# Routing the last token group in two halves, the other groups ahead of the last projections

## The reference

```python
# linear attention, 16 heads of 16, 64 features a head
q_prime = relu(q @ Wqf.T); k_prime = relu(k @ Wkf.T)
kv = einsum('bhnf,bhne->bhfe', k_prime, v)
out = einsum('bhmf,bhfe->bhme', q_prime, kv) / (qk_sum + 1e-8)
x = x + out @ Wo.T + bo
# mixture of experts on layernorm(x): 32 experts, top 6
scores = softmax(x2d @ wg_router.T)
topk_w, topk_idx = top_k(scores, 6)
pos = cumsum(one_hot(flat_idx)) - 1          # place of a token in its expert
xe = zeros(E, C, D).at[flat_idx, pos].add(x_rep)
ye = (silu(xe @ w_gate) * (xe @ w_up)) @ w_down
y = sum over k of ye[...] * topk_w  +  shared expert(x2d)
```

## Time and profile before

| | |
|---|---|
| median of 3 runs | 2223.54 us (2222.8 to 2228.28) |
| profiled execution | 2246.44 us |
| its span, first to last instruction | 2244.7 us |
| busy: PE, DVE, ACT, POOL | 1942.7, 1366.5, 1076.1, 718.4 us |
| mean granted TensorE clock | 0.929 |
| the last three groups of the LA | 784 to 967 us |
| last DVE instruction of the LA to the first gate product | 966.55 to 978.46 us |

### The profile page before, as it was taken

How to read it: one execution, slowest core, us unless ns; L and a number is a source line. 1 busy time by engine, 2 the same in 40 slices (tenths; PEclk the granted TensorE clock), 3 DMA queues, 4 the chain that set the end, 5 groups by cost and what they waited for, 6 DMA issues and landing times. The chain is left out here.

```text
span 2244.7 us, 41989 instructions
## 1 busy us (share of the span) xinstructions
PE 1942.7 (87%) x11797; PEld 1302.7 (58%) x11798; DVE 1366.5 (61%) x3452; ACT 1076.1 (48%) x2800; POOL 718.4 (32%) x691
## 2 busy tenths in 40 slices
PE   7999999998998999977899999889766789888655
PEld 4666666665555666644676666545433457677433
DVE  6555656665776344545343344679789447777687
ACT  5545545453333222102344444367588337666575
POOL 3332332330000014451465556523100026566310
PEclk9999999999999888878999999999888889899787
DMA  8960000000000001151678776400010111111100
GB/s 305 307 185 0 0 0 0 0 1 0 0 0 1 1 15 60 57 187 63 143 167 170 166 175 116 102 1 2 11 49 1 65 34 33 31 38 31 31 17 22
DMA packets 145575, 145.10 MB, mean 65 GB/s; under 512 B 49376, under 2 KB 133568, under 8 KB 145344
## 3 DMA queue, kind: packets, MB, share of 16 engines
q1 hardware_dynamic: 122432, 113.81, 17.1%
q0 software_dynamic: 23040, 30.01, 7.8%
HBM read 137.12 MB, written 66.44 MB: 91 GB/s over the span
## 5 line engine op out<-in xcount | busy, mean ns | idle before, releaser
L1686 POOL DMA_INDIRECT expert_sums<-moe_rows_in,moe_to x128 | 198.0, 1547 | 151.6 <-DMA expert_sums<-moe_rows_in,moe_to 79.2
L1949 DVE COPY moe_ht_e<-moe_turned 128x256 f32<-128x256 f32 x128 | 54.4, 425 | 203.3 <-PE moe_turned L1767 178.3
L1759 PE MATMUL moe_gate<-moe_places,moe_xt 128*128 x512 | 175.9, 466 | 2.1 <-issue 1.9
L619 ACT ACTIVATE ga_prob<-ga_score,ga_neg_max 128x128 f32<-128x128 f32 x256 | 99.8, 392 | 145.7 <-DVE ga_neg_max L493 145.7
L3012 POOL TENSOR_TENSOR wa_low<-wa_low,wa_top 128x512 f32<-128x512 f32 x128 | 133.2, 1041 | 97.7 <-DVE wa_top L3216 96.4
L240 POOL TENSOR_TENSOR ga_q_inv<-ga_q_sum,half 128x4 f32<-128x4 f32 x64 | 64.5, 1008 | 304.2 <-DVE ga_q_sum L476 304.2
L2039 POOL TENSOR_TENSOR ln_rstd<-ln_var,half 128x4 f32<-128x4 f32 (+1 forms) x16 | 21.9, 1370 | 370.8 <-DVE ln_var L2035 370.7
L1153 POOL DMA_INDIRECT slot_x<-early x96 | 94.3, 982 | 115.2 <-DVE early L1144 76.8
L3213 DVE SCALAR_TENSOR_TENSOR wa_low<-wa_score,early 128x512 f32<-128x512 f32 x128 | 87.8, 686 | 61.1 <-PE wa_score L3052 58.6
L375 PE MATMUL ga_summed<-ga_wo,ga_out_t 128*128 128x256 f32 x512 | 122.5, 383 | 0.7 <-ACT ga_out_t L627 0.7
L375 PEld LDWEIGHTS ga_summed<-ga_wo,ga_out_t 128*128 128x128 f32 x512 | 98.1, 192 | 40.6 <-issue 29.2
(11 more groups left out here) (480 smaller groups left out, 4969.4 us busy)
## 6 DMA issues: line engine op xcount, KB each, us to landing
moe_places<-in_L_ffn_packed SPq DMA_DIRECT2D x128, 608.0 KB
slot_x<-zeros SPq DMA_DIRECT2D x24, 1076.0 KB, 14.9
moe_rows_in<-slot_x SPq DMA_DIRECT2D x128, 134.5 KB
wa_v<-v_ctx SPq DMA_DIRECT2D x16, 180.0 KB, 3.0
early<-in_L_xattn_Wq SPq DMA_DIRECT2D x5, 512.0 KB, 7.8
x<-in_x SPq DMA_DIRECT2D x4, 512.0 KB, 9.3
ga_wo<-in_L_xattn_Wo SPq DMA_DIRECT2D x1, 2048.0 KB, 14.3
expert_sums<-zeros SPq DMA_DIRECT2D x2, 1024.0 KB, 8.6
```

The lines of the kernel that those rows point to most:

```text
L619: last = act.activation(prob[:, n % 2, part], score[:, n % 2, part], ACT.Exp, bias=neg_max[:, n % 2, h:h + 1], accum_out=total[:, n % 2, h ...
L1686: pool.indirect_dma_start(out=mem.sums[j % SUMS], out_offset=bass.IndirectOffsetOnAxis(ap=to[:, j:j + 1], axis=0), in_=y[:, j, :], in_offs ...
L1759: last = pe.matmul(both[j % 2][:, 0:2 * FE], xt[:, j % 2, c, :], packed[:, place, c * 2 * FE:(c + 1) * 2 * FE].rearrange("p a n -> p (a n) ...
```

## The change

- The last group's routing is split in spans of two tiles: `SPANS` has the three groups of four tiles and two of two tiles each (tiles 12, 13 and tiles 14, 15). All steps of the router take a span where they took a group.
- The first half of the last group is scaled after the last `normalize` of the LA, ahead of the last `update`; PE transposes it ahead of the last `sum_up` and computes its logits behind it; DVE softens it at the end of the LA. Its `exp`, `choose`, `pick`, `rank` and `find_slots` stand at the head of MoE, beside the second half's transposes and logits. The second half's `rank` stands after u = 1, and its `find_slots` after the first multiplication.
- In the other groups, transposes come after f = 0 and f = 1 (before: 3 and 5), the logits after f = 4 (before: behind all projections), `exp` on ACT after the Relu of f = 6 (before: after the last), `choose` ahead of the first tile's values, `pick` behind the first tile's pairs and `find_slots` behind the second's (before: `choose`, `pick`, `find_slots` behind the pairs of the tiles 0, 1 and 2).
- `EARLY_ROWS` is 11 instead of 10: POOL scatters eleven tiles in the LA. The root of tiles 12 and 13 stands ahead of tile 10's scatters, that of tiles 14 and 15 behind them.

The diff, cut; the steps left out only take the span's size in place of `GROUP`:

```diff
-EARLY_ROWS = (GROUPS - 1) * GROUP - 2
+EARLY_ROWS = (GROUPS - 1) * GROUP - 1
+SPANS = [(g * GROUP, (g + 1) * GROUP) for g in range(GROUPS - 1)] + [(B - GROUP, B - GROUP // 2), (B - GROUP // 2, B)]
+SPAN_OF = [n for n, (a, b) in enumerate(SPANS) for t in range(a, b)]
...
     def group(self, a, g):
-        return a[:, g * GROUP:(g + 1) * GROUP]
+        return a[:, SPANS[g][0]:SPANS[g][1]]
...
     def root(self, pool, g):
-        a, b = g * GROUP, (g + 1) * GROUP
+        a, b = SPANS[g]
         pool.wait_ge(self.var_ready.sem, self.var_ready.at(g))
-        pool.tensor_tensor(self.rstd[:, a:b], self.var[:, a:b], self.mem.half[:, 0:GROUP], ALU.pow).then_inc(self.rooted.sem, 1)
...
-        if n >= 2:
-            pe.wait_ge(self.lated.sem, self.lated.at(n // 2 - 1))
+        if GROUP <= 2 * n < B - GROUP // 2:
+            pe.wait_ge(self.lated.sem, self.lated.at(SPAN_OF[2 * n] - 1))
...
     def logits(self, pe, g):
-        pe.wait_ge(self.moved.sem, self.moved.at(2 * g + 1))
+        a, b = SPANS[g]
+        pe.wait_ge(self.moved.sem, self.moved.at(b // 2 - 1))
         if g >= 1:
-        for i in range(GROUP):
-            t = g * GROUP + i
+        for i in range(b - a):
+            t = a + i
...
-        pe.wait_ge(self.moved.sem, self.moved.at(2 * g + 1))
-        out = self.pairs[:, 0:GROUP * NE]
+        a, b = SPANS[g]
+        pe.wait_ge(self.moved.sem, self.moved.at(b // 2 - 1 if b <= B - GROUP else B // 2 - 1))
+        if b == B:
+            pe.wait_ge(self.lated.sem, self.lated.at(g - 1))
+        out = self.pairs[:, 0:(b - a) * NE]
...
+        if t in [a for a, b in SPANS]:
+            pool.wait_ge(self.placed.sem, self.placed.at(SPAN_OF[t]))
         if 1 <= t <= EARLY_ROWS:
             pool.wait_ge(self.mem.scattered[(t - 1) % SCATTERS].sem, 16 * TOPK * ((t - 1) // SCATTERS + 1))
...
                 for t in range(EARLY_ROWS):
                     if t % TG == 1 and t // TG < G - 2:
                         router.root(pool, t // TG + 1)
+                    if t == EARLY_ROWS - 1:
+                        router.root(pool, G - 1)
                     router.scatter(pool, t)
-                router.root(pool, G - 1)
+                router.root(pool, G)
...
                         m, part = divmod(f, FC // HC)
                         pe.wait_ge(moved.sem, moved.at(t * NP + m))
                         project(t, 2 * HC + f, [(w.fq[:, part * P:(part + 1) * P], qt[:, m, :])])
-                        if g >= 0 and f == 3:
+                        if g >= 0 and f == 0:
                             router.turn(pe, 2 * g)
-                        if g >= 0 and f == 5:
+                        if g >= 0 and f == 1:
                             router.turn(pe, 2 * g + 1)
-                    if g == 0:
-                        pe.wait_ge(route_loaded.sem, 16)
-                    if g >= 0:
-                        router.logits(pe, g)
+                        if g == 0 and f == 4:
+                            pe.wait_ge(route_loaded.sem, 16)
+                        if g >= 0 and f == 4:
+                            router.logits(pe, g)
...
                             turn_row(t * TG + j)
                         if j >= 1:
                             turn_mixed(t, j - 1)
-                        if g >= 0 and j == 2:
+                        if g >= 0 and j == 1:
                             router.rank(pe, g)
                     sum_up(t, TG - 2)
                     mix_up(t, TG - 1)
                     turn_mixed(t, TG - 1)
+                    if t == G - 1:
+                        router.turn(pe, 2 * t)
                     sum_up(t, TG - 1)
+                    if t == G - 1:
+                        router.logits(pe, t)
...
-                        if g >= 0 and n == 2 * HC + 3:
+                        if g >= 0 and n == 2 * HC:
                             router.move(act, 2 * g)
-                        if g >= 0 and n == 2 * HC + 5:
+                        if g >= 0 and n == 2 * HC + 1:
                             router.move(act, 2 * g + 1)
-                    if g >= 0:
-                        router.exp(act, g)
+                        if g >= 0 and n == 2 * HC + 6:
+                            router.exp(act, g)
...
+                    if t == G - 1:
+                        router.move(act, 2 * t)
...
                     for j in range(TG):
                         if g >= 0 and j == 0:
                             router.soften(dve, g)
+                            router.choose(dve, g)
                         features_values(t, j)
                         if j >= 2:
                             update(t, j - 2)
+                        if t == G - 1 and j == TG - 1:
+                            dve.wait_ge(counted.sem, counted.at(t * TG + 1))
+                            router.variance(dve, t)
                         if j >= 1:
                             normalize(t, j - 1)
                         pairs(t, j)
                         if g >= 0 and j == 0:
-                            router.choose(dve, g)
+                            router.pick(dve, g)
                         if g >= 0 and j == 1:
-                            router.pick(dve, g)
-                        if g >= 0 and j == 2:
                             router.find_slots(dve, g)
                     update(t, TG - 2)
                     normalize(t, TG - 1)
+                    if t == G - 1:
+                        router.shifts(dve, t)
+                        router.scale(dve, t)
                     update(t, TG - 1)
                 dve.wait_ge(counted.sem, counted.at(B - 1))
-                router.variance(dve, G - 1)
-                router.shifts(dve, G - 1)
-                router.scale(dve, G - 1)
+                router.variance(dve, G)
+                router.soften(dve, G - 1)
+                router.shifts(dve, G)
+                router.scale(dve, G)
...
-                router.turn(pe, 2 * LASTG)
                 router.turn(pe, 2 * LASTG + 1)
-                router.logits(pe, LASTG)
+                router.logits(pe, LASTG + 1)
+                router.rank(pe, LASTG)
                 pe.wait_ge(loaded.sem, 16 * len(loads))
                 for u in range(U):
                     gate_up(u)
                     if u == 1:
-                        router.rank(pe, LASTG)
+                        router.rank(pe, LASTG + 1)
                         router.counts(pe)
...
-                router.move(act, 2 * LASTG)
+                router.exp(act, LASTG)
                 router.move(act, 2 * LASTG + 1)
-                router.exp(act, LASTG)
+                router.exp(act, LASTG + 1)
...
-                router.soften(dve, LASTG)
                 router.choose(dve, LASTG)
                 router.pick(dve, LASTG)
+                router.soften(dve, LASTG + 1)
+                router.find_slots(dve, LASTG)
+                router.choose(dve, LASTG + 1)
+                router.pick(dve, LASTG + 1)
                 for u in range(U):
                     multiply(u)
                     if u == 0:
-                        router.find_slots(dve, LASTG)
+                        router.find_slots(dve, LASTG + 1)
```

More of the change, by code:

```diff
@@ L1048, in scale @@
     def scale(self, dve, g):
-        for t in range(g * GROUP, (g + 1) * GROUP):
+        for t in range(*SPANS[g]):
             dve.tensor_scalar(self.mem.xn[:, t, 0:H], self.mem.x[:, t, :], self.rstd[:, t:t + 1], self.shift[:, t:t + 1],
@@ L1094, in choose @@
         self.then(dve, dve.reciprocal(total, total))
-        self.then(dve, dve.tensor_tensor(prob, prob, total.unsqueeze(2).to_broadcast([P, GROUP, NE]), ALU.mult))
-        for t in range(g * GROUP, (g + 1) * GROUP):
+        self.then(dve, dve.tensor_tensor(prob, prob, total.unsqueeze(2).to_broadcast([P, size, NE]), ALU.mult))
+        for t in range(*SPANS[g]):
             n = self.did(dve.max(self.top[:, t, :], self.prob[:, t, :]))
         dve.wait_ge(self.step.sem, n)
-        for t in range(g * GROUP, (g + 1) * GROUP):
+        for t in range(*SPANS[g]):
             n = self.did(dve.max_index(self.index[:, t, :], self.top[:, t, :], self.prob[:, t, :]))
@@ L1127, in find_slots @@
     def find_slots(self, dve, g):
-        ranks = self.pairs[:, 0:GROUP * NE].rearrange("p (t e) -> p t e", e=NE)
-        slot, lanes = self.group(self.slot, g), self.lane[:, :].unsqueeze(1).to_broadcast([P, GROUP, NE])
+        size = SPANS[g][1] - SPANS[g][0]
+        ranks = self.pairs[:, 0:size * NE].rearrange("p (t e) -> p t e", e=NE)
+        slot, lanes = self.group(self.slot, g), self.lane[:, :].unsqueeze(1).to_broadcast([P, size, NE])
+        chosen, product = self.chosen[:, :, 0:size, :], self.product[:, :, 0:size, :]
         slot_f = self.group(self.slot_f, g)
```

35 lines of the change are left out of this document (19 added, 16 removed).

## The result

The kernel after the change takes 2237.41 us (median of 4 runs, 2233.71 to 2239.8), the one before 2223.85 us (4 runs, 2222.8 to 2228.28): 13.6 us slower. The recorded ratio, which is estimated from all the runs and is not the quotient of the two medians, is 1.0052 [1.0034, 1.0070], or 11.6 us. The forecast was 6.2 us slower, with 2236 as the end of its range.

A forecast was written before the change was run, and what follows sets the result against it. PE was taken as the seldom idle engine, the LA's end and the way to the first shared gate product as the path, dispatch having slack. Terms 6.0 − 1.9 + 1.0 + 1.1 = +6.2: 2229.7 us, range 2215 to 2236.

The forecast's parts named there:

- Forecast +6.0: Tail of the LA: its end moves from 966.55 to 972.5 us, 6.0 later, including the loop's 4.4.
- POOL's queue decides its end: Tail of the LA: scatters and roots on POOL end last, 2.2 us behind the rival chain through the variance.
- the 2.6, 1.3 and 0.5 of the forecast: LA loop: later table load and VectorE work cost PE 2.6, 1.3, 0.5 us for t = 1, 2, 3; sum 4.4.
- The drain: LA, t = 1: by the skill page, 1.4 us more behind the table load, making the whole sum 7.6.
- The two terms for the clock: Wider PE gaps keep its clock low longer: +1.0 us behind the head of MoE, +1.1 in the LA.
- Forecast -1.9: Head of MoE: less router work on PE brings the first shared gate product 1.9 us earlier, bounds 3.1 and 0.
- the 10.0: Head of MoE: shared weights taken as landed 10.0 us after the LA's end, against 11.9 to the first gate product before.
- the 15.5 us of "remote": Shared expert: two ACT stalls before Silu cost PE 15.5 us in the profiled execution; timed runs probably hold no such stall.
- Rival 1: MoE: scatter stream and stalls belong together, the change could remove them; all gone, -9.3 us, 2214; chance 0.2.
- Rivals 2 and 3: 2: nothing reaches PE, 2224 to 2227 us, chance 0.15. 3: clock makes it dearer, up to +16, chance 0.15.
- rival 2: LA and head: DVE's shifts absorbed, head saves POOL's extra cost; +0.5 to +3 us, chance 0.15.

The follow-up runs named there:

- e3: Changed kernel with ten tiles scattered in the LA instead of eleven, both last roots behind tile 9: 2257.59 us, ratio 1.0073 to the kernel before.
- e2: Kernel before with only the new order of the other groups: 2247.15 us, ratio 1.0019.
- e5: Changed kernel unaltered, measured and profiled again: 2252.25 us, ratio 1.0029 to the kernel before.
- e7: Changed kernel with every tile's scatters waiting until the tile before has landed, in MoE too: 2227.07 us, ratio 0.9918 to the kernel before.
- e11: Kernel before with the new order of the other groups and the wait for the tile before at every tile: 2226.97 us, ratio 0.9920.
- e0: Kernel before, unchanged, measured and profiled again: 2243.51 us, ratio 0.9997.
- e1: Changed kernel with the other groups' order put back, halves and eleventh tile kept: 2261.00 us, ratio 1.0074 to the kernel before.
- e4: Kernel before with the last group's halves alone, old order of the other groups, ten tiles scattered in the LA: 2260.19 us, ratio 1.0064.
- e6: Kernel before with every tile's scatters waiting until the tile before has landed, in MoE too: 2228.71 us, ratio 0.9911.
- e9: Kernel before with every tile waiting for the tile before, plus a wait after each tile's third scatter except tiles 8 and 9: 2224.63 us, ratio 0.9897.
- e10: Kernel before with the last group's halves alone and the wait for the tile before at every tile: 2234.69 us, ratio 0.9951.
- e8: Kernel before with no tile's scatters waiting for the tile before, in the LA neither: 2271.37 us, ratio 1.0117.

## Why the prediction was right, and where not

The direction was right. By the medians the time was 7.7 us too low, beyond the end of the range by 1.4; by the ratio the kernel after lies at 2235.1 on the scale of the forecast's 2223.54, just inside it. Part of the agreement is luck: a term in the head had the wrong sign, a stage was left out, and with the scatters held back the change isn't visibly slower at all.

**The LA: the sum right, its parts not all.** Forecast +6.0, measured +5.3 (241.16 - 235.88). POOL's queue decides its end, as forecast: two roots with tile 10's scatters between, and DVE waits 3.93 us for the second, where 2 were expected. e3, without the eleventh tile, shows this wait gone. The loop came out near its terms, if one counts from the first projection of t = 1, which stands at 784.15 before and 779.48 after:

```profile
784.15 4.49 PE L1284 MATMUL la_proj<-xnt,la_wq 128*128 128x512 f32 x8
...
805.43 1.97 PE L1314 MATMUL la_pair<-la_v,la_kf 128*128 128x34 f32 x16 [0.84 <-DVE la_kf L1440]
...
924.32 2.25 PE L1314 MATMUL la_pair<-la_v,la_kf 128*128 128x34 f32 x16 [0.86 <-DVE la_kf L1440]
```

```profile
779.48 4.47 PE L1298 MATMUL la_proj<-xnt,la_wq 128*128 128x512 f32 x8
```

To the first pair product of t = 1, 2 and 3 it is 21.28, 79.64 and 140.17 us before and 23.34, 83.46 and 143.81 after: +2.1, +1.8 and -0.2, in all 3.6, for the 2.6, 1.3 and 0.5 of the forecast. The first two repeat: to t = 1 and t = 2 it is 23.3 to 23.4 and 83.4 to 83.5 us in all six profiles with the new order (after, e2, e3, e5, e7, e11), and 20.7 to 21.3 and 78.5 to 80.0 in all seven with the old order and the waits in the LA (before, e0, e1, e4, e6, e9, e10). The third is lost in the stalls. From there to the end the tail costs 3.2 more (42.23 and 45.40), and the stretch ahead of that first projection was 1.5 shorter; e6 and e0, two executions with the code of before in that stretch, differ by as much in it. In three pieces, with the first pair product of t = 3 as the second cut (us):

| | order | halves | tiles | ahead of t = 1 | to the pair product of t = 3 | to the end of the LA |
|---|---|---|---|---|---|---|
| before | old | no | 10 | 53.5 | 140.2 | 42.2 |
| e6 | old | no | 10 | 51.9 | 144.5 | 45.0 |
| after | new | yes | 11 | 52.0 | 143.8 | 45.4 |
| e7 | new | yes | 11 | 51.9 | 145.2 | 43.9 |
| e3 | new | yes | 10 | 53.5 | 145.2 | 41.0 |
| e10 | old | yes | 10 | 53.5 | 141.4 | 48.8 |
| e1 | old | yes | 11 | 49.8 | 143.3 | 54.2 |

The last column follows POOL's queue, as the forecast has it. In e1 tile 8's first scatter starts 25.3 us behind the pair product, in after 16.6, that is 8.7 later, and the piece is 8.8 longer.

The drain that the Trainium skill adds to a load ("ScalarE: Activation LUTs", "What ACT_TABLE_LOAD costs") isn't seen here: the load ends at 797.03 + 1.28 = 798.31, and `exp` starts at 798.33. The two terms for the clock, +1.0 behind the head and +1.1 in the LA, aren't seen: without stalls the shared expert takes 73.2 to 73.8 us with the halves (after, e7, e10) and 73.0 and 74.1 without (e11, e6), and the mean granted clock of the LA is 0.86 before and 0.85 after.

**The head of MoE: wrong.** Forecast -1.9, measured +1.35. The mechanism was right, PE waits for the weights (3.30). But I kept the 4.06 us from the end of the LA to their request, and it became 5.37; and they were not there after 10.0 us but after 13.3. In e5 and e7 the head took 12.5 and 12.2, with waits of 2.6 and 2.4 us for the same DMA, and with ten tiles in the LA 12.2 (e3) and 10.8 (e4). The step that failed is the 10.0: for the request I had one row, and the landing was worked out from bytes moved, not from a wait, since before nothing waited for it. In its place the runs show a request at 5.37 and a landing at 13.3. The later request goes with the halves: it stands 4.06 us behind the LA's end in each of the seven profiles without them and 4.71 to 5.37 in each of the seven with them. By what means isn't shown.

**Behind the shared expert: missed.** The stretch from the end of the expert loop to the next attention is 57.8, 58.2 and 57.2 us in after, e5 and e7, and 53.4, 53.7 and 54.4 in before, e0 and e6. I had nothing there. POOL's accumulating scatters end later against PE's loop: the last one starts 9.0, 9.2 and 8.8 us behind the loop's end in the first three and 4.7, 4.4 and 4.8 in the others, and the attention begins 47.6 to 50.0 us behind it in every profile. e9, which has no halves, shows 56.9, and e10, which has them, 53.1, so it isn't a cost of the halves as such; why the scatters end later is open.

**The stalls: the assumption that failed.** I took the 15.5 us of "remote" as a matter of that one execution, since the timed runs were 22.9 us shorter, and carried the difference over to the median. Their size was about right, 16.9 us. But in the later sets the timed runs of before (2230.71 to 2258.29) have medians 15 to 18 us above that of the same kernel with the wait at every tile (17.7 where both ran on one chip), so most of them probably hold such stalls. Rival 1 had the cause, that the scatter stream and the stalls belong together, and the wrong consequence: the change doesn't remove them; the kernel after had none in its first profile and 17.86 and 7.18 us of ACT in its second. What goes with its halves is that they fall ahead of the owners' product, where PE waits 13.7 to 17.0 us in each of the four executions with halves that had them in MoE. Rivals 2 and 3: nothing of a +16 from the clock is seen; with the stream held back, e7 fits rival 2, no change, though it can't exclude the forecast's 6.2 us.

**What stays open.** How the 13.6 us on the chip of the result come about. Against the profile of before without its 16.9 us of stalls, after is 8.7 us longer, and 6.6 of these are in the LA and the head. The stretches that the change touches, LA to the next attention without the shared expert, are together 13.7 us longer, but one pair of profiles can't carry that. With the stream held back the two kernels can't be told apart, and their LA and head are equal (253.3 against 253.1), where e6 had 9 us of remote waits in its LA and e7 half of one. The first chip's median of before, 2223.85, is even below that of e6, 2228.71, so its timed runs perhaps held few stalls; no kernel with the wait ran on that chip, and it can't be seen in the times.

## What to carry to other kernels

A wait that the profile puts down to something remote, and that appears in some executions only, must be tied to what runs beside it before a change is costed around it: here one condition that holds back the scatters of each tile was worth 0.9%, more than the whole change cost. When parts of a change each measure slower than the whole, look for a disturbance whose place they move, take it away, and measure them again. A cost that one profile shows can be checked cheaply in the others: the same distance between two rows, in every profile that has the edit and every one that hasn't. And of a queue that only issues transfers, ask not only whether it ends in time but what it does to the others while it is full.

## What the runs showed of the hardware

- While GpSimd issued indirect scatters 1.28 us apart and didn't wait in between (eighteen or more in a row), VectorE and ScalarE took up results of TensorE late, by 11.3 us at the first stall of e8; the idle times that the profile puts down to "remote" there are up to 24.23 us. With a wait of about 2.4 us for the landing after each six, such waits were up to 13.11 us, and in the LA alone (e6, e7, e10, e11 have none in MoE); after each three (six for two tiles) there were none (e9). No profile of the fourteen has one of over 0.5 us ahead of the first of these scatters or later than 6 us behind the start of the last; the 128 accumulating scatters of the expert loop, some 2.7 us apart, came with none. TensorE worked on meanwhile until it needed the late result; in e8 its own signal for the logits is recorded at 865.06, with the product's modelled end at 853.80. That the scatters cause it is shown by e6, e8 and e9, by what means is not: the kernels vary how many scatters follow each other, and no record tells how many were open at a time.
- It doesn't happen each time: the kernel after issued 30 scatters in a row in MoE (from 975.18 us) without any such wait in its first profile, and had two of ScalarE and one of VectorE in its second.
- The same kernel had medians of 2223.85, 2243.37, 2246.39 and 2246.71 us in four sets of runs.
